# Attention's projections in three 16-bit passes, layer norm by four batches, value halves added in PSUM

## The chip, the cores and the metric

One core of a Trainium2 chip runs the whole kernel. The metric is the device time of one execution in microseconds, the median of the runs. TensorE (PE) multiplies matrices into PSUM, VectorE (DVE), ScalarE (ACT) and GpSimd (POOL) do the rest, SyncE (SP) issues the DMAs. Each engine works through its own list in order and waits on semaphores.

## The reference

```python
x = x + tanh(g_xattn[0]) * xattn(layernorm(x), ctx_768, Wq, Wk, Wv, Wo)
x = x + tanh(g_ffn[0]) * ffn(layernorm(x), W1, b1, W2, b2)

# xattn: 16 heads of 16
q, k, v = x @ Wq, context @ Wk, context @ Wv
out = softmax(q k^T / 4 (masked)) v        # per head
return out @ Wo
# ffn: ternary weights, exact gelu
h = gelu(x @ ternary(W1).T + b1); return h @ ternary(W2).T + b2
```

x is 128 batches x 128 rows x 256, the context 128 x 128 x 192, the hidden width of the feed-forward part 1024. Everything is float32.

## The kernel before

The attention stage takes two batches as a group (class Group), 64 groups in all; a loop body holds two groups, of parity 0 and 1. The feed-forward stage follows and takes four batches a step. The order on each engine is written out by hand: pe_group (L436), act_group (L625), dve_group (L834), pool_group (L917) and sp_group (L233) give each engine's list for one group, and interleave the end of one group, the middle of this one and the projections of later ones.

A group on TensorE is made of slots. A slot has rough_scores of four heads (L328, q against k with 16 rows), from which VectorE takes a maximum for each row (take_max, L744); scores of four heads (L352, 50 rows: high and low halves and the maximum), from which ScalarE makes exponentials (L596) and GpSimd their low half (L914); and weigh of four heads (L372 high and L373 low half of the probabilities, against v16 with 33 columns: 16 of the high half of v, 16 of its low half and a column of ones). Between them stand the projections in fp32, q (L296) and k (L305) of the group after next, v (L312) of the next one, in a bank that all three share (pj_bank), and the output projection (L391) of each batch. The transposes of x (L275), of the context (L285, L287), of the row maxima (transpose_max, L338) and of the attention output (L381) and the output projection share another bank, tr_bank; each waits until the bank's last content was read.

ScalarE copies the transposed tiles to SBUF (copy_xT L539, copy_ctxT L546, copy_attnT L604) and makes the 16-bit high halves of q, k and v (L559, L567, L576); VectorE makes the low halves (L707, L714, low_v L735). At the end of a group ScalarE's list has copy_attnT of the group's first batch and then high_v of the next group; project_out of that batch comes in the next group, after rough scores, scores and weigh of one slot. VectorE sums and scales the weighed values (read_weighed L773 and L774, normalise L782), once for each half of the heads, and adds the projected output to the residual (add_attention, L789).

The layer norm is worked out in 14 parts (ln_part, L657), spread over dve_group: statistics (bn_stats, L668), an inverse root by three Newton steps on columns of two numbers, a shift. It runs once for each group of two batches. The feed-forward stage uses the same function by four batches.

## Time and profile before

| | us |
|---|---|
| median of three runs | 1853.07 (1853.0 to 1859.49) |
| span of the profiled execution, first to last instruction | 1838.7 |
| PE busy | 1761.7 |
| DVE busy | 1538.3 |
| ACT busy | 952.2 |
| POOL busy | 661.2 |

The profile is of one execution. A run's time includes what lies before the first and behind the last instruction, so its median stands 14.4 us above the span of the profiled execution. Matmuls are pipelined: a row's length is that of the instruction from its start to the end of its result, and the pace is read from one start to the next. The timeline merges like instructions that follow one another ("x4"). The granted clock is the share of its full 2.4 GHz that TensorE was given.

### The profile page before, as it was taken

The numbers are of one execution on the slowest core, as the hardware profiler recorded it, in microseconds if no ns is written. First come the engines' busy times: TensorE is split into PE (matmuls) and PEld (weight loads), VectorE is DVE, ScalarE is ACT, GpSimd is POOL, SyncE is SP. The second block draws the span as 40 slices with busy tenths as digits, with TensorE's granted clock in tenths as the row PEclk, the third lists the DMA queues.
The fourth block names the chain that finished last, engine by engine and source line by source line (L and its number), as shares of the span: only waits on it lengthen the run. The fifth ranks groups of instructions, "written<-read, shape, count | busy, mean of one in ns | idle before, by whom it ended". The sixth has DMA issues, their size and how long they took to land.

```text
span 1838.7 us, 47676 instructions
## 1 busy us (share of the span) xinstructions
PE 1761.7 (96%) x14501; PEld 1152.8 (63%) x14501; DVE 1538.3 (84%) x4375; ACT 952.2 (52%) x1799; POOL 661.2 (36%) x809
## 2 busy tenths in 40 slices
PE   6999999999999999999999999999799999999998
PEld 3666666666666666666666666666466666666665
DVE  6799798898888988888898888987788888888886
ACT  3455555554555555555555555544455555555554
POOL 2344454454444444444444444545211111111111
PEclk9699898898988988898898888987699999999999
DMA  3222222222222222222222222221101110001011
GB/s 98 59 65 74 55 64 68 60 64 69 59 59 59 74 59 59 74 59 59 69 64 59 71 58 59 75 53 36 50 24 35 34 34 31 26 34 34 34 34 47
DMA packets 170607, 101.13 MB, mean 55 GB/s; under 512 B 20817, under 2 KB 170321, under 8 KB 170577
## 3 DMA queue, kind: packets, MB, share of 16 engines
q1 hardware_dynamic: 170576, 100.75, 20.0%
q8 instruction: 17, 0.28, 0.1%
q14 instruction: 14, 0.11, 0.0%
HBM read 32.53 MB, written 16.78 MB: 27 GB/s over the span
## 4 chain that ended last, share of the span: by engine, by line
PE 84%; DVE 8%; issue 5%; ACT 2%; DVEq 0%; DMA 0%; ACTq 0%
PE bank L1059 11%; PE bank L312 10%; PE bank L352 9%; PE bank L328 9%; PE bank L305 8%; PE bank L391 8%; PE bank L296 8%; PE bank L372 5%; PE bank L1089 5%; PE bank L1088 5%; PE bank L373 2%; PE bank L381 2%; DVE smax L759 2%; DVE y L1046 2%; PE bank L285 1%
## 5 line engine op out<-in xcount | busy, mean ns | idle before, releaser
L914 POOL TENSOR_TENSOR probl<-prob 128x512 f16<-128x512 f32 x512 | 531.6, 1044 | 712.5 <-ACT prob L596 710.9
L596 ACT ACTIVATE prob<-bank,masks 128x512 f32<-128x512 f32 x512 | 344.6, 686 | 314.3 <-PE bank L352 301.8
L744 DVE TENSOR_REDUCE smax<-bank 128x4 f32<-128x512 f32 x512 | 348.5, 682 | 46.1 <-PE bank L328 46.0
L1075 DVE TENSOR_TENSOR hidl<-hid 128x512 f16<-128x512 f32 x256 | 226.7, 886 | 79.4 <-ACT hid L1070 78.7
L1059 PE MATMUL bank<-y,w1T 128*128 128x512 f16 x1024 | 263.0, 379 | 29.7 <-DVE y L1046 28.2
L1070 ACT ACTIVATE hid<-bank,b_sb 128x512 f32<-128x512 f32 x256 | 175.8, 687 | 212.2 <-PE bank L1059 205.9
L1088 PE MATMUL bank<-w2T,hid 128*128 128x256 f16 x1024 | 237.4, 273 | 1.4 <-ACT w2T L1003 1.4
L1089 PE MATMUL bank<-w2T,hidl 128*128 128x256 f16 x1024 | 237.4, 273 | 0.0
L1153 POOL TENSOR_TENSOR xres<-xres,b2g 128x1024 f32 (+1 forms) x32 | 75.5, 2361 | 431.3 <-ACT yln L1023 413.4
L328 PEld LDWEIGHTS bank<-k_rows,q_rows 16*128 16x128 f16 x2048 | 120.5, 96 | 160.2 <-issue 128.2
L352 PE MATMUL bank<-q_rows,k_rows 50*128 50x128 f16 x2048 | 216.5, 230 | 0.9 <-DMA q_rows<-smaxT 0.9
L328 PE MATMUL bank<-k_rows,q_rows 16*128 16x128 f16 x2048 | 213.7, 227 | 1.7 <-DVE smax L744 1.7
L312 PE MATMUL bank<-wv_sb,ctxT 128*128 128x256 f32 (+1 forms) x512 | 195.7, 486 | 0.9 <-DVE k L714 0.9
L372 PE MATMUL bank<-v,prob 128*128 128x33 f16 x2048 | 178.2, 183 | 0.1
L373 PE MATMUL bank<-v,probl 128*128 128x33 f16 x2048 | 170.5, 179 | 0.0
L391 PE MATMUL bank<-wo_sb,attnT 128*128 128x256 f32 x512 | 166.7, 455 | 1.1 <-ACT attnT L604 1.1
L296 PE MATMUL bank<-xlnT,wq_sb 128*128 128x256 f32 x512 | 164.2, 451 | 2.0 <-DVE v L735 1.3
L372 PEld LDWEIGHTS bank<-v,prob 128*128 128x128 bf16 x2048 | 126.6, 98 | 59.9 <-issue 13.4
L1059 PEld LDWEIGHTS bank<-y,w1T 128*128 128x128 f16 x1024 | 97.5, 98 | 103.9 <-issue 33.1
L352 PEld LDWEIGHTS bank<-q_rows,k_rows 50*128 50x128 f16 x2048 | 121.9, 98 | 60.6 <-issue 12.6
L305 PE MATMUL bank<-ctxT,wk_sb 128*128 128x256 f32 (+1 forms) x512 | 159.0, 418 | 0.8 <-ACT ctxT L547 0.8
L373 PEld LDWEIGHTS bank<-v,probl 128*128 128x128 f16 x2048 | 131.2, 98 | 0.3 <-issue 0.3
(88 smaller groups left out, 2645.0 us busy)
## 6 DMA issues: line engine op xcount, KB each, us to landing
q_rows<-q SPq DMA_DIRECT2D x384, 64.0 KB, 2.6
k_rows<-k SPq DMA_DIRECT2D x384, 64.0 KB, 2.5
xres<-in_x_dram SPq DMA_DIRECT2D x64, 256.0 KB, 2.8
out_dram<-ystage SPq DMA_DIRECT2D x32, 512.0 KB, 2.9
ctx_sb<-in_ctx_dram SPq DMA_DIRECT2D x64, 192.0 KB, 2.9
q_rows<-smaxT SPq DMA_DIRECT2D x128, 8.0 KB
w_raw<-in_L_ffn_W_dram SPq DMA_DIRECT2D x2, 1024.0 KB, 6.6
prob<-in_L_xattn_Wq_dram SPq DMA_DIRECT2D x1, 256.0 KB, 4.0
```

What stands on the lines that cost most here:

```text
L312: last = pe.matmul(pj_bank[:, b * D:(b + 1) * D], ctxT[g.parity][0:rows, k, b * S:(b + 1) * S], wv_sb[0:rows, k, :], start=(k == 0), stop= ...
L328: last = pe.matmul(sm_bank[u % 2][:, c * S:(c + 1) * S], q_rows[g.parity][0:HD, b, u * UH + c, :], k_rows[g.parity][0:HD, b, u * UH + c, : ...
L352: last = pe.matmul(st_bank[u % 2][:, c * S:(c + 1) * S], k_rows[g.parity][0:SR, b, u * UH + c, :], q_rows[g.parity][0:SR, b, u * UH + c, : ...
L372: pe.matmul(o, high, v, start=True, stop=False)
L373: last = pe.matmul(o, probl[u][:, c * S:(c + 1) * S], v, start=False, stop=True)
L391: last = pe.matmul(tr_bank[:, 0:D], attnT[:, k, :], wo_sb[:, k, :], start=(k == 0), stop=(k == KD - 1))
L596: act.activation(prob[u][:], st_bank[u % 2][:], ACT.Exp, bias=0.0, scale=masks[g.parity][:, 2 + b:3 + b]).then_inc(exp_done, 1)
L744: dve.tensor_reduce(smax[:, b, u * UH:(u + 1) * UH], sm_bank[u % 2][:].rearrange("p (h j) -> p h j", h=UH), AX.X, ALU.max).then_inc(max_ta ...
L914: pool.tensor_tensor(probl[u][:], prob[u][:], prob[u][:].bitcast(BF16)[:, 1::2], ALU.subtract).then_inc(prob_split, 1)
L1059: last = pe.matmul(h_bank[f % 2][:], w1T[:, k, f * P:(f + 1) * P], y16[g.parity][:, part, k, :], start=(i == 0), stop=(i == 2 * KD - 1))
L1088: pe.matmul(o, high, w2T[:, f, :], start=(f == 0 and b % 2 == 0), stop=False, skip_group_check=True)
L1089: last = pe.matmul(o, hidl[f % HBUF][:, b * S:(b + 1) * S], w2T[:, f, :], start=False, stop=(f == FB - 1), skip_group_check=True)
```

## The change

- The four projections take 16-bit high and low halves of both operands, in three passes (high x high, high x low, low x high), where one fp32 matmul stood. The weights are scaled by 64 and split once, ahead of the first group (high_weights on ScalarE, low_weights on VectorE). The context is cut as 96 + 96 rows, not 128 + 64.
- ScalarE's copies of the transposed x, context and attention output now write the high half; VectorE writes the low half (low_x, low_ctx, low_attn). The projections, and whoever uses tr_bank next, wait for the low half.
- low_q and low_k are one instruction each, not two; q and k lie in PSUM by batch.
- weigh multiplies each half of the probabilities by each half of v, to the same 17 columns of PSUM: four matmuls a head of 17, 16, 17 and 16 columns, not two of 33. One bank holds a whole batch, so VectorE reads it once a batch (sum_weighed, normalise) and the reduction over the halves is gone.
- The layer norm of x runs once for two groups, by four batches, in groups of parity 0; x is loaded by four batches.
- The order of pe_group and act_group stays. In dve_group low_attn of the last group's first batch stands behind norm(0) at the start.

```diff
+            if g.parity == 1 and left >= 6:
+                sp.wait_ge(ln_ready, x_past)
+                load_x(sp, g.half + 3)
             if left >= 3:
...
+        def by_batch(m):
+            return pj_bank[:].rearrange("p (b m s) -> p m b s", m=KD, b=2)[:, m]
         def project_q(pe, g, m):
             if m == 0:
-                pe.wait_ge(xT_copied, g.n + 1)
+                pe.wait_ge(xT_split, g.n + 1)
             for k in range(KD):
-                last = pe.matmul(pj_bank[:, m * T:(m + 1) * T], wq_sb[:, k, m * P:(m + 1) * P],
-                                 xlnT[:, k, :], start=(k == 0), stop=(k == KD - 1))
+                for i, (wp, xp) in enumerate(SPLIT):
+                    last = pe.matmul(by_batch(m), wq16[:, wp, k, m * P:(m + 1) * P],
+                                     xT16[:, xp, k, :].rearrange("p (b s) -> p b s", b=2),
+                                     start=(k == 0 and i == 0 and m == 0), stop=(k == KD - 1 and i == 2),
+                                     skip_group_check=True)
             if m == KD - 1:
                 last.then_inc(q_made, 1)
...
         def project_v(pe, g, b):
-            for k, rows in enumerate((P, C1)):
-                last = pe.matmul(pj_bank[:, b * D:(b + 1) * D], ctxT[g.parity][0:rows, k, b * S:(b + 1) * S],
-                                 wv_sb[0:rows, k, :], start=(k == 0), stop=(k == 1))
+            for k in range(2):
+                for i, (wp, xp) in enumerate(SPLIT):
+                    last = pe.matmul(pj_bank[:, b * D:(b + 1) * D], ctxT16[g.parity][:, xp, k, b * S:(b + 1) * S],
+                                     wv16[:, wp, k, :], start=(k == 0 and i == 0 and b == 0),
+                                     stop=(k == 1 and i == 2), skip_group_check=True)
             if b == 1:
                 last.then_inc(v_made, 1)
...
                 pe.wait_ge(v_split, g.n + 1)
-            if u % 2 == 0 and not (isinstance(n, int) and n == 0):
-                pe.wait_ge(norm_read, n * 2 + (half - 1))
+            if u == 0 and not (isinstance(n, int) and n < 2):
+                pe.wait_ge(norm_done, n - 1)
             for c in range(UH):
-                o = pv_bank[half][:, (c0 + c) * VC:(c0 + c + 1) * VC]
-                v = v16[g.parity][:, b, u * UH + c, :]
+                h = u * UH + c
+                o = pv_bank[b][:, h * VH:(h + 1) * VH]
                 high = prob[u][:].bitcast(BF16)[:, 2 * c * S + 1:2 * (c + 1) * S:2]
-                pe.matmul(o, high, v, start=True, stop=False)
-                last = pe.matmul(o, probl[u][:, c * S:(c + 1) * S], v, start=False, stop=True)
+                low = probl[u][:, c * S:(c + 1) * S]
+                vh, vl = v16[g.parity][:, b, h, 0:VH], v16[g.parity][:, b, h, VH:VC]
+                pe.matmul(o, high, vh, start=(h == 0), stop=False, skip_group_check=True)
+                pe.matmul(o[:, 0:HD], high, vl, start=False, stop=False, skip_group_check=True)
+                pe.matmul(o, low, vh, start=False, stop=False, skip_group_check=True)
+                last = pe.matmul(o[:, 0:HD], low, vl, start=False, stop=(h == HEADS - 1), skip_group_check=True)
             last.then_inc(weighed, 1)
...
         def project_out(pe, n, tr_free):
             for busy in tr_free:
                 pe.wait_ge(*busy)
-            pe.wait_ge(attnT_copied, n + 1)
+            pe.wait_ge(attnT_split, n + 1)
             for k in range(KD):
-                last = pe.matmul(tr_bank[:, 0:D], attnT[:, k, :], wo_sb[:, k, :], start=(k == 0),
-                                 stop=(k == KD - 1))
+                for i, (wp, xp) in enumerate(SPLIT):
+                    last = pe.matmul(tr_bank[:, 0:D], attnT16[:, xp, k, :], wo16[:, wp, k, :],
+                                     start=(k == 0 and i == 0), stop=(k == KD - 1 and i == 2))
             last.then_inc(projected, 1)
             return [(x1_done, n + 1)]
...
         def copy_ctxT(act, g):
             act.wait_ge(ctx_transposed, g.n + 1)
             if not (isinstance(g.half, int) and g.n < 2):
                 act.wait_ge(v_made, g.n - 1)
-            act.copy(ctxT[g.parity][:, 0, :], tr_bank[:, 0:T])
-            act.copy(ctxT[g.parity][0:C1, 1, :], tr_bank[0:C1, T:2 * T]).then_inc(ctxT_copied, 1)
...
+        def high_weights(act):
+            act.wait_ge(weights_in, 16 * 4)
+            for i, (raw, w) in enumerate(((wq_raw, wq16), (wk_raw, wk16), (wv_raw, wv16), (wo_raw, wo16))):
+                for k in range(2):
+                    if i >= 2:
+                        last = act.activation(w[:, 0, k, :], raw[:, k, :], ACT.Identity, bias=0.0, scale=WS)
+                        continue
+                    for m in range(KD):
+                        last = act.activation(permuted(w[:, 0, k], m), permuted_raw(raw[:, k], m), ACT.Identity,
+                                              bias=0.0, scale=WS)
+                last.then_inc(weights_high, 1)
...
+        def norm_x(dve, half, parts):
             for i in parts:
                 if i == 0:
-                    dve.wait_ge(x_in[g.parity], 16 * (g.half + 1))
-                if i == 3 and not (isinstance(g.half, int) and g.n == 0):
-                    dve.wait_ge(ln_done, 2 * g.n)
-                rows = [row_of(g.batch(b)) for b in range(2)] if i == 0 else (None,) * 2
-                ln_part(dve, i, rows, ln_step, g.n * (LN_PARTS - 1), ln_ready)
+                    dve.wait_ge(x_in, 16 * (half + 1))
+                if i == LN_PARTS - 2 and not (isinstance(half, int) and half == 0):
+                    dve.wait_ge(ln_done, QB * half)
+                rows = [row_of(half * QB + b) for b in range(QB)] if i == 0 else ()
+                ln_part(dve, i, rows, ln_step, half * (LN_PARTS - 1), ln_ready)
...
+        def low_x(dve, g):
+            dve.wait_ge(xT_high, g.n + 1)
+            dve.tensor_tensor(xT16[:, 1].rearrange("p k t -> p (k t)"), tr_bank[:],
+                              xT16[:, 0].rearrange("p k t -> p (k t)"), ALU.subtract).then_inc(xT_split, 1)
+        def low_ctx(dve, g):
+            dve.wait_ge(ctxT_high, g.n + 1)
+            dve.tensor_tensor(ctxT16[g.parity][:, 1].rearrange("p k t -> p (k t)"), tr_bank[0:CK, :],
+                              ctxT16[g.parity][:, 0].rearrange("p k t -> p (k t)"),
+                              ALU.subtract).then_inc(ctxT_split, 1)
+        def low_attn(dve, n):
+            dve.wait_ge(attnT_high, n + 1)
+            dve.tensor_tensor(attnT16[:, 1].rearrange("p k t -> p (k t)"), tr_bank[:, 0:KD * S],
+                              attnT16[:, 0].rearrange("p k t -> p (k t)"), ALU.subtract).then_inc(attnT_split, 1)
...
         def low_q(dve, g):
             dve.wait_ge(q_high, g.n + 1)
-            for b in range(2):
-                last = dve.tensor_tensor(q16[g.parity][:, 1, b], by_batch(pj_bank)[:, b], q16[g.parity][:, 0, b],
...
+        def low_weights(dve):
+            for i, (raw, w) in enumerate(((wq_raw, wq16), (wk_raw, wk16), (wv_raw, wv16), (wo_raw, wo16))):
+                dve.wait_ge(weights_high, i + 1)
+                for k in range(2):
+                    if i >= 2:
+                        last = dve.scalar_tensor_tensor(w[:, 1, k, :], raw[:, k, :], WS, w[:, 0, k, :], ALU.mult,
+                                                        ALU.subtract)
+                        continue
+                    for m in range(KD):
+                        last = dve.scalar_tensor_tensor(permuted(w[:, 1, k], m), permuted_raw(raw[:, k], m), WS,
+                                                        permuted(w[:, 0, k], m), ALU.mult, ALU.subtract)
+                last.then_inc(weights_split, 1)
...
+        def sum_weighed(dve, n, b):
+            dve.wait_ge(weighed, (n + 1) * UNITS)
             if not (isinstance(n, int) and n < 2):
                 dve.wait_ge(attn_transposed, n - 1)
-            pv = pv_bank[half][:, 0:HB * VC].rearrange("p (h c) -> p h c", h=HB)
-            dve.reciprocal(rsum[:, b, heads], pv[:, :, 2 * HD])
-            dve.tensor_reduce(attn[b][:, heads, :],
-                              pv[:, :, 0:2 * HD].rearrange("p h (two d) -> p h d two", two=2), AX.X,
-                              ALU.add).then_inc(norm_read, 1)
-        def normalise(dve, n, b, half):
-            heads = slice(half * HB, (half + 1) * HB)
-            dve.wait_ge(norm_read, n * 2 + (half + 1))
-            dve.tensor_tensor(attn[b][:, heads, :], attn[b][:, heads, :],
-                              rsum[:, b, heads].unsqueeze(2).to_broadcast([P, HB, HD]),
+            dve.reciprocal(rsum[:, b, :], pv_of(b)[:, :, HD]).then_inc(norm_read, 1)
+        def normalise(dve, n, b):
+            dve.wait_ge(norm_read, n + 1)
+            dve.tensor_tensor(attn[b][:], pv_of(b)[:, :, 0:HD],
+                              rsum[:, b, :].unsqueeze(2).to_broadcast([P, HEADS, HD]),
                               ALU.mult).then_inc(norm_done, 1)
...
-            norm_x(dve, g1, range(LN_PARTS))
+            low_x(dve, g0)
+            low_weights(dve)
             low_q(dve, g0)
             dve.wait_ge(gates_set, 1)
+            dve.tensor_scalar(gates[:, 0:1], gates[:, 2:3], 1.0 / WS, None, ALU.mult).then_inc(gate_scaled, 1)
+            low_ctx(dve, g0)
             low_k(dve, g0)
-            norm_x(dve, g0.after(2), range(0, LN_AHEAD))
+            low_x(dve, g1)
+            norm_x(dve, 1, range(0, LN_PARTS - 2))
             low_v(dve, g0)
-            norm_x(dve, g0.after(2), range(LN_AHEAD, LN_PARTS))
+            norm_x(dve, 1, range(LN_PARTS - 2, LN_PARTS))
+            low_ctx(dve, g1)
             low_q(dve, g1)
...
             first = isinstance(g.half, int) and g.n == 0
-            g1, g2, g3, g4 = (g.after(k) for k in range(1, 5))
+            g1, g2 = g.after(1), g.after(2)
             def norm(i):
                 if left == 0:
-                    norm_y(dve, Group(0, 0), ((i - LN_AHEAD) % LN_PARTS,))
-                if i < LN_AHEAD and left >= 4:
-                    norm_x(dve, g4, (i,))
-                if i >= LN_AHEAD and left >= 3:
-                    norm_x(dve, g3, (i,))
+                    norm_y(dve, Group(0, 0), (i,))
+                if g.parity == 0 and left >= 4:
+                    norm_x(dve, g.half + 2, (i,))
+            norm(0)
+            if not first:
+                low_attn(dve, g.batch(0) - 2)
             take_max(dve, g, 1, 2)
-            norm(8)
             if not first:
                 add_attention(dve, g.batch(0) - 2)
-            norm(9)
+            norm(1)
             take_max(dve, g, 1, 3)
             round_max(dve, g, 1)
-            norm(10)
+            norm(2)
             low_max(dve, g, 1)
+            norm(3)
             if not first:
-                read_weighed(dve, g.batch(0) - 1, 1, 1)
-                normalise(dve, g.batch(0) - 1, 1, 1)
-            norm(11)
+                sum_weighed(dve, g.batch(0) - 1, 1)
+                norm(4)
+                normalise(dve, g.batch(0) - 1, 1)
+            else:
+                norm(4)
             if left >= 2:
+                low_ctx(dve, g2)
                 low_q(dve, g2)
-            norm(12)
+            norm(5)
             if left >= 1:
                 take_max(dve, g1, 0, 0)
-            norm(13)
+            norm(6)
             if left >= 1:
                 take_max(dve, g1, 0, 1)
-            read_weighed(dve, g.batch(0), 0, 0)
-            normalise(dve, g.batch(0), 0, 0)
+            norm(7)
+            if not first:
+                low_attn(dve, g.batch(0) - 1)
             if left >= 1:
                 take_max(dve, g1, 0, 2)
+            norm(8)
             if left >= 2:
                 low_k(dve, g2)
+            norm(9)
             if not first:
                 add_attention(dve, g.batch(0) - 1)
+            norm(10)
             if left >= 1:
                 take_max(dve, g1, 0, 3)
                 round_max(dve, g1, 0)
+                norm(11)
                 low_max(dve, g1, 0)
-            norm(0)
-            read_weighed(dve, g.batch(0), 0, 1)
-            norm(1)
-            normalise(dve, g.batch(0), 0, 1)
-            norm(2)
+            else:
+                norm(11)
...
             if left >= 1:
                 take_max(dve, g1, 1, 1)
-            norm(4)
-            read_weighed(dve, g.batch(1), 1, 0)
...
```

## Rows read from the trace of the kernel before

**Rows 1.** The page: busy shares of the span, and the granted clock in 40 slices.

```profile
PE 1761.7 (96%) x14501; PEld 1152.8 (63%) x14501; DVE 1538.3 (84%) x4375; ACT 952.2 (52%) x1799; POOL 661.2 (36%) x809
...
PEclk9699898898988988898898888987699999999999
```

**Rows 2.** Timeline of TensorE (start us, length us, engine, line, operation): L338.

```profile
587.45 0.23 PE L338 MATMUL bank<-ident,smax 128*32 128x128 f16 x1
...
642.01 0.23 PE L338 MATMUL bank<-ident,smax 128*32 128x128 f16 x1
...
666.11 0.23 PE L338 MATMUL bank<-ident,smax 128*32 128x128 f16 x1
...
684.19 0.23 PE L338 MATMUL bank<-ident,smax 128*32 128x128 f16 x1
...
706.89 0.23 PE L338 MATMUL bank<-ident,smax 128*32 128x128 f16 x1
```

**Rows 3.** Windows (stretch, length; busy of PE, PEld, DVE, ACT, POOL; clock; DMA).

```profile
586.00:650.80 64.80, 63.86 (x626) 41.47 (x625) 58.74 (x168) 37.90 (x76) 32.10 (x45) 1.00 0.25 65
650.80:664.50 13.70, 13.70 (x72) 8.46 (x72) 9.43 (x33) 3.83 (x9) 4.02 (x4) 0.50 0.22 63
695.20:705.40 10.20, 10.20 (x51) 6.58 (x51) 7.12 (x22) 3.35 (x8) 3.12 (x3) 0.50 0.31 84
1330.00:1830.00 500.00, 471.37 (x3281) 321.18 (x3282) 411.61 (x1122) 267.88 (x440) 73.19 (x31) 1.00 0.09 32
```

**Rows 4.** Timeline of TensorE, 603 to 610 us, full clock.

```profile
603.62 1.03 PE L296 MATMUL bank<-xlnT,wq_sb 128*128 128x256 f32 x4
...
604.58 0.39 PE L328 MATMUL bank<-k_rows,q_rows 16*128 16x128 f16 x4
...
606.81 2.48 PE L305 MATMUL bank<-ctxT,wk_sb 128*128 128x256 f32 x8
...
609.22 0.39 PE L328 MATMUL bank<-k_rows,q_rows 16*128 16x128 f16 x4
```

**Rows 5.** Timeline of TensorE, two matmuls of one weigh, six steps apart.

```profile
618.32 0.18 PE L373 MATMUL bank<-v,probl 128*128 128x33 f16 x1
...
618.47 0.18 PE L373 MATMUL bank<-v,probl 128*128 128x33 f16 x1
```

**Rows 6.** Timeline of TensorE in the feed-forward stage, matmuls seven steps apart.

```profile
1505.51 0.27 PE L1088 MATMUL bank<-w2T,hid 128*128 128x256 f16 x1
...
1506.27 0.27 PE L1089 MATMUL bank<-w2T,hidl 128*128 128x256 f16 x1
```

**Rows 7.** Timeline of TensorE, ScalarE and VectorE, 616 to 620 us.

```profile
616.47 1.22 PE L312 MATMUL bank<-wv_sb,ctxT 128*128 128x256 f32 x4
...
617.62 0.39 PE L328 MATMUL bank<-k_rows,q_rows 16*128 16x128 f16 x4
...
617.87 0.85 ACT L576 ACTIVATE v<-bank,masks 128x256 f16<-128x256 f32 x2 [0.81 <-PE bank L312]
...
618.49 1.11 PE L391 MATMUL bank<-wo_sb,attnT 128*128 128x256 f32 x4
...
618.75 0.88 DVE L735 SCALAR_TENSOR_TENSOR v<-bank,masks,v 128x256 f16<-128x256 f32 x2 [0.53 <-ACT v L576]
...
619.53 0.39 PE L328 MATMUL bank<-k_rows,q_rows 16*128 16x128 f16 x4
```

**Rows 8.** Groups of instructions by line and shape (count; busy us, mean ns; idle before).

```profile
L668 DVE BATCH_NORM_STATS2 stats<-xres 128x6 f32 x228 | 82.4, 413 | 0.0
...
L1046 DVE TENSOR_TENSOR y<-bank,y 128x512 f16<-128x512 f32 x64 | 40.9, 677 | 0.1
```

**Rows 9.** Timeline of TensorE at L338, with the idle time before it.

```profile
692.61 0.22 PE L338 MATMUL bank<-ident,smax 128*32 128x128 f16 x1 [0.35 <-DVE smax L759]
```

**Rows 10.** Timeline of TensorE at half clock: four rough scores, then four scores.

```profile
697.22 0.60 PE L328 MATMUL bank<-k_rows,q_rows 16*128 16x128 f16 x4
...
697.75 0.60 PE L352 MATMUL bank<-q_rows,k_rows 50*128 50x128 f16 x4
```

More of the change, by code:

```diff
@@ L657, in ln_part @@
         def ln_part(dve, i, rows, step, base, ready):
-            n = len(rows)
-            half, y, t, shift = (rstd[:, k, 0:n] for k in range(4))
+            half, y, t = (rstd[:, k, :] for k in range(3))
             if i > 0:
@@ L1010, in norm_y @@
             for i in parts:
[L1011 to L1014 removed]
+                if i == LN_PARTS - 2:
+                    if isinstance(g.half, int) and g.n == 0:
+                        dve.wait_ge(ln_done, B)
+                    else:
+                        dve.wait_ge(y_done, QB * g.n)
+                rows = [row_of(g.n * QB + b) for b in range(QB)] if i == 0 else ()
                 ln_part(dve, i, rows, y_step, g.n * (LN_PARTS - 1), y_ready)
```

216 lines of the change are left out of this document (107 added, 109 removed).

## The prediction

> **What bounds the kernel now.** I read the page first: TensorE is busy for 96% of the span, VectorE for 84%, and the granted TensorE clock is below full in most slices of the first two thirds, full in the last third [rows 1]. The attention stage fills about 1270 us of the span, as 64 groups of two batches. Then I read the timeline of TensorE at one instruction that comes once in a group, the transpose of the row maxima at L338 (it has two a group, so every second one stands there). Three groups in a row take 587.45 to 642.01, 18.19 us each, at full clock. The next takes 24.10 us, and one soon after 22.70 us; six groups take 119.44 us, 19.91 each [rows 2]. The view by windows says what the long ones are: for 13.70 us (650.80 to 664.50) and 10.20 us (695.20 to 705.40) the granted clock is 0.50, that is 1.2 GHz in place of 2.4, with TensorE busy all the time; the feed-forward stage, denser 256 and 512 column matmuls, holds 1.00 throughout [rows 3]. So a group is bounded by TensorE's own in-order stream, and a drop of the clock costs (24.10 - 18.19) = 5.9 and (22.70 - 18.19) = 4.5 us, 1.7 us a group over six groups. VectorE is no bound as a sum, but it runs its list in order, and TensorE waits for single items of it.
>
> **TensorE's work, removed.** One project_q half (four fp32 matmul instructions) takes 603.62 to 604.58, 0.96 us; project_k 606.81 to 609.22, 2.41 [rows 4]; one project_v half 616.47 to 617.62, 1.15, and one project_out 618.49 to 619.53, 1.04 [rows 7]. A group has two q halves, one k, two v halves and two outputs: 1.92 + 2.41 + 2.30 + 2.08 = 8.7 us. The change makes them 48 passes of 256 columns on 16-bit data. Such a pass stands in the feed-forward stage: seven in a row start 0.76 us apart, 109 ns each [rows 6]. 48 x 0.109 = 5.2 us, and I add 0.1 us at each of seven ends, because project_out's 1.04 us are 0.17 more than its eight 109 ns column passes and part of that is the changeover to a matmul with other rows. So 5.9, a saving of **2.8 us a group**. Bounds: 3.5 without changeover, 2.3 with 0.17 each.
>
> **TensorE's work, added.** weigh has 8 matmuls of 33 columns for four heads now, and will have 16 of 17 or 16 columns. The present ones start 25 ns apart (618.32 to 618.47 for six steps) [rows 5], although 33 columns at 2.4 GHz are 14 ns: the step is not set by columns, so halving the columns brings nothing. 8 more x 25 ns x 8 units = **1.6 us a group**. Bounds: 1.6, and 0.9 if a step fell to the 14 ns. Net of both: -1.2 us a group. That is all the gain there is, some 75 us over the stage.
>
> **VectorE's work.** It loses two reductions and half of its small instructions on [128 x 8] sums a batch, and half of the Newton steps, since four batches share them; it gains low_x and low_ctx (512 columns from PSUM, as the 677 ns of the row at L1046 [rows 8]) and two low_attn (256 columns, about 0.42). As a sum it gets lighter, so it is nothing on the path. What counts is where the new items stand.
>
> **The new wait.** project_out now waits for attnT_split, which low_attn gives, and low_attn of a group's first batch stands in VectorE's list behind low_v of the same point and, in every even group, behind the four bn_stats of norm(0). low_v waits for high_v on ScalarE, and that for project_v. Follow this in the trace: project_v ends at 617.62, high_v starts at 617.87, low_v at 618.75 and takes 0.88 [rows 7]; low_attn adds 0.42 and the signal 0.1. From the end of project_v: 0.25 + 0.88 + 0.88 + 0.42 + 0.1 = 2.5 us. In even groups four bn_stats of 413 ns [rows 8], back to back some 0.34 each, make it 3.9. TensorE needs it much sooner: today project_out starts 618.49 - 617.62 = 0.87 us after project_v, and with the longer weigh 1.07. So it stands idle for 1.45 us in odd groups and 2.85 in even ones, **2.15 us a group**; before, the copy on ScalarE that fed it came ahead of high_v. Behind the waiting instruction are the rough scores and scores that feed VectorE's maxima and ScalarE's exponentials, so nothing of the next slot can fill the hole. Bounds: 1.1 if low_v were already further on, 3.0 if one small instruction more stretches. A smaller wait of the same kind: transpose_max stands idle already, 0.35 us at 692.61 for VectorE's low half of the maxima [rows 9]; low_x of 0.68 comes behind it and gives the bank free, and low_ctx does the same for the other transpose_max. weigh's added time hides part; I take 0.6 us a group for the two (bounds 0 and 1.3). Loads of x come as four batches in half as many DMAs and are early; they cost nothing.
>
> **Sum at full clock:** 18.19 - 1.2 + 2.15 + 0.6 = 19.7 us a group.
>
> **The clock.** The falls come where TensorE's stream is thin: the one at 695.20 [rows 3] follows, by 2.6 us, on the idle time at L338 [rows 9], with the 16-row rough scores and the 33-column matmuls between. The change thins exactly that place: an idle stretch of 1.45 to 2.85 us beside rough scores and 17-column matmuls, and the projections, the densest part, shrink from 8.7 to 5.9 us. Two groups in six meet a fall today; I expect one in every group. A fall costs 0.43 us per us at half clock today (5.9 of 13.7); with more waiting in the stream, which the clock doesn't stretch, I take 4.3 us a group. 19.7 + 4.3 = **24.0 us a group**. Against 19.91: 4.1 x 62 groups (the first two run while the pipeline fills) = 254 us. The start adds the scaling and splitting of all four weight matrices on ScalarE and VectorE before the first project_q, some 24 instructions of about 0.3 us, partly beside each other: 6 us. The feed-forward stage is unchanged. Span 1838.7 + 260 = 2099; the median of the runs is 14.4 us above the span of the profiled execution, so **2113 us**.
>
> **Rivals.**
> 1. The wait comes, the clock doesn't fall oftener. For: TensorE is 98 to 100% busy in the stage today and its clock falls all the same, so idle time isn't the sole trigger; the walk doesn't say what is. Against: what is thinned is what precedes the falls. Price: 19.7 + 1.7 = 21.4 a group, +1.5 x 62 + 6 = +99: **1952**. Beside this the Trainium skill (TensorE: Matmul & The Clock Gate, "Why this matters for your kernels") blames drops on idle gaps between bursts longer than any wait worked out here, which would give this case; the trace disagrees with it as the only cause, for the clock is 0.50 right after a stretch with 63.86 of 64.80 us busy [rows 3].
> 2. The clock, once down, stays down for most of the stage, since 16-bit projections leave no stretch as dense as fp32's. A group wholly at half clock: rough and real scores 16 x 0.53 (697.22 to 697.75 [rows 10]) = 8.5, projections 5.9 x 1.9 = 11.2, weigh 3.9, transposes 3.8, waits 1.0: 28.4. (28.4 - 19.91) x 62 + 6 = +532: **2385**. Today it recovers within 14 us, in q's or the fp32 stretches.
> 3. The wait is hidden and the sum of TensorE's work decides: -1.2 x 62 + 6 = -68: **1785**. It would take low_v finishing some 1.5 us sooner after project_v than the 2.0 us that the trace shows; I find nothing that gives that.
> 4. Saving, wait and clock cancel: within 0.5% of 1853.
>
> **How the numbers follow.** Chances: forecast 0.58 (2000 to 2240 by its bounds), rival 1 0.17, rival 2 0.13, rival 3 0.08, rival 4 0.04. The range 1880 to 2300 leaves out rivals 3 and 4 and most of rival 2. Faster by over 0.5% (what a measurement can tell from no change) 0.08, within 0.04, slower 0.88.
>
> **What would show it.** In the profile after: project_out idle before its first matmul, released by VectorE's low_attn, 1 to 3 us a time, longer in every second group; weigh's matmuls 25 ns apart; projection passes 109 ns apart at full clock; the granted clock at 0.50 for 30 to 60% of the attention stage. I am wrong if the mean granted clock there stays near 0.90 (today 23.9 of 119.44 us at half), or if project_out starts without idle time.

## The result and the profile after

The changed kernel takes **2220.88 us** (2201.32 to 2225.24, four runs) against 1853.03 for the kernel before on the same chip: a ratio of 1.199, 95% interval [1.192, 1.205]. The forecast was 2113 in a range of 1880 to 2300, slower.

First the page of the changed kernel, the lines that answer to [rows 1].

```profile
span 2214.9 us, 55976 instructions
...
PE 2050.9 (93%) x19621; PEld 1404.8 (63%) x19621; DVE 1378.3 (62%) x3549; ACT 974.8 (44%) x1747; POOL 660.0 (30%) x809
...
PEclk9555555555555566655555555556556999999999
```

VectorE's busy time fell by 160 us, and TensorE's rose by 289. The granted clock, mostly 8 to 9 tenths before, reads 5, in some slices 6, in the attention stage; the feed-forward stage at the end is as it was. The windows say it in numbers (stretch, length; busy of PE, PEld, DVE, ACT, POOL; clock; DMA); the first five lie each within a single stretch at one level of the clock and all but fill it, then come 1000 us of the stage and the feed-forward stage.

```profile
100.60:110.90 10.30, 9.77 (x153) 7.34 (x152) 8.91 (x23) 6.88 (x13) 5.78 (x9) 1.00 0.16 41
110.90:151.80 40.90, 38.15 (x358) 25.69 (x358) 20.36 (x53) 14.74 (x27) 12.22 (x16) 0.50 0.19 53
343.00:411.20 68.20, 63.42 (x603) 42.87 (x602) 36.16 (x99) 25.61 (x47) 21.16 (x27) 0.50 0.18 46
619.50:622.80 3.30, 3.30 (x59) 2.71 (x59) 2.63 (x7) 2.46 (x6) 0.93 (x1) 1.00 0.01 2
623.00:674.00 51.00, 48.24 (x455) 32.17 (x452) 25.80 (x68) 19.17 (x36) 16.91 (x23) 0.50 0.20 49
150.00:1150.00 1000.00, 939.80 (x9839) 645.95 (x9838) 565.98 (x1432) 418.73 (x775) 348.02 (x465) 0.59 0.19 48
1705.00:2213.00 508.00, 475.98 (x3322) 324.54 (x3319) 415.60 (x1128) 270.48 (x443) 73.53 (x32) 1.00 0.10 33
```

For comparison the kernel before over the same 1000 us:

```profile
150.00:1150.00 1000.00, 988.30 (x8733) 637.55 (x8732) 856.55 (x2508) 527.74 (x1054) 452.94 (x602) 0.90 0.24 63
```

Before, the clock went to 0.50 for 10 to 14 us at a time and was back; now it is at 0.50 for 41 or 51 us at most times, once for 68, and back at 1.00 for 10 or 3. A mean of 0.59 is 1.2 GHz for (1 - 0.59) / 0.5 = 82% of the stage. From one transpose of row maxima to the next but one (L354, the measure of [rows 2]) a group takes 25.9 us on average over 56 groups (19.8 before), with none under 22.8.

The timeline of the changed kernel at the end of an odd group (parity 1), at half clock, shows the wait that the prediction worked out; it answers to [rows 7].

```profile
713.26 1.49 PE L327 MATMUL bank<-wv,ctxT 96*128 96x256 f16 x6
...
714.92 0.85 ACT L599 ACTIVATE v<-bank,masks 128x256 f16<-128x256 f32 x2 [1.04 <-PE bank L327]
...
715.80 0.88 DVE L799 SCALAR_TENSOR_TENSOR v<-bank,masks,v 128x256 f16<-128x256 f32 x2 [3.19 <-ACT v L599]
...
716.60 1.40 DVE L701 BATCH_NORM_STATS2 stats<-xres 128x6 f32 x4
...
717.91 0.41 DVE L752 TENSOR_TENSOR attnT<-bank,attnT 128x256 f16<-128x256 f32 x1
...
718.37 1.46 PE L411 MATMUL bank<-wo,attnT 128*128 128x256 f16 x6 [2.03 <-DVE attnT L752]
```

project_v (L327) ends at 714.68, where the next rough scores (L344) start; high_v (L599) ends at 715.77, low_v (L799) at 716.68, the four bn_stats (L701), grouped in one line, at 718.00, low_attn (L752) at 718.32, and project_out starts at 718.37 after 2.03 us of idle time. From 714.68 that is 3.69 us, where 3.9 was worked out. In the other groups, without bn_stats, the same place reads:

```profile
688.44 0.88 DVE L799 SCALAR_TENSOR_TENSOR v<-bank,masks,v 128x256 f16<-128x256 f32 x2 [3.20 <-ACT v L599]
...
689.23 0.41 DVE L752 TENSOR_TENSOR attnT<-bank,attnT 128x256 f16<-128x256 f32 x1
...
689.70 1.46 PE L411 MATMUL bank<-wo,attnT 128*128 128x256 f16 x6 [0.72 <-DVE attnT L752]
```

Idle times of 0.72 and 2.03 us alternate through the whole stage. In total (engine and line that waited, whom for; us in total, times, longest):

```profile
PE bank L411 <- DVE attnT L752: 86.1, 65, 2.0
...
PE bank L354 <- DVE xT L741: 9.2, 23, 1.1
```

The other terms can be read off as well. weigh's matmuls, 14 steps apart at full clock, then 13 steps apart at half clock (start, length):

```profile
101.21 0.17 PE L390 MATMUL bank<-v,prob 128*128 128x16 f16 x1
...
101.56 0.17 PE L392 MATMUL bank<-v,probl 128*128 128x16 f16 x1
```

```profile
706.64 0.17 PE L390 MATMUL bank<-v,prob 128*128 128x16 f16 x1
...
706.98 0.18 PE L391 MATMUL bank<-v,probl 128*128 128x17 f16 x1
```

25 ns a step at full clock, as the 33 columns were [rows 5], and 26 to 27 at half. Here the Trainium skill (TensorE: Matmul & The Clock Gate, "Wait — 56ns, not 53.3ns?") states that starts are never closer than about 25 ns however few the columns; the trace agrees for 16, 17 and 33 columns at full clock, and between the two levels of the clock the step of 16 and 17 columns moves by 1 to 2 ns only. The projection of k, twelve passes of 256 columns, first at full and then at half clock:

```profile
103.15 1.48 PE L317 MATMUL bank<-ctxT,wk 96*128 96x256 f16 x12
104.56 0.39 PE L344 MATMUL bank<-k_rows,q_rows 16*128 16x128 f16 x4
```

```profile
699.92 2.77 PE L317 MATMUL bank<-ctxT,wk 96*128 96x256 f16 x12
702.62 0.60 PE L344 MATMUL bank<-k_rows,q_rows 16*128 16x128 f16 x4
```

1.41 us and 2.70 us, 0.117 and 0.225 a pass with the changeover. The fp32 form took 2.41 at full clock [rows 4]. So both terms of TensorE's own work came out as summed: the projections got shorter, weigh longer.

### The profile page after: what moved, and what is told of

Its sections match the earlier page's. It is cut to its first block, busy times and chain, and to the rows that moved or that the text cites. A ratio compares the mean times of both kernels' runs of the same rounds, so it can differ in the third digit from the quotient of the medians.

```text
span 2214.9 us, 55976 instructions
## 1 busy us (share of the span) xinstructions
PE 2050.9 (93%) x19621; PEld 1404.8 (63%) x19621; DVE 1378.3 (62%) x3549; ACT 974.8 (44%) x1747; POOL 660.0 (30%) x809
## 4 chain that ended last, share of the span: by engine, by line
PE 77%; DVE 10%; issue 8%; ACT 3%; DVEq 1%; DMA 0%; ACTq 0%; SPq 0%
PE bank L344 9%; PE bank L1123 9%; PE bank L368 8%; PE bank L305 7%; PE bank L327 7%; PE bank L411 6%; PE bank L317 6%; PE bank L1152 4%; PE bank L1153 4%; PE bank L389 4%; PE bank L400 3%; PE bank L290 2%; PE bank L391 2%; PE bank L279 2%; PE bank L390 2%
## 5 line engine op out<-in xcount | busy, mean ns | idle before, releaser
L344 PE MATMUL bank<-k_rows,q_rows 16*128 16x128 f16 x2048 | 281.0, 281 | 1.8 <-DVE smax L808 1.8
L368 PE MATMUL bank<-q_rows,k_rows 50*128 50x128 f16 x2048 | 280.4, 281 | 0.7 <-DMA q_rows<-smaxT 0.7
L389 PEld LDWEIGHTS bank<-v,prob 128*128 128x128 bf16 x2048 | 209.9, 103 | 87.9 <-issue 73.5
L344 PEld LDWEIGHTS bank<-k_rows,q_rows 16*128 16x128 f16 x2048 | 158.4, 117 | 165.2 <-issue 152.8
L389 PE MATMUL bank<-v,prob 128*128 128x17 f16 x2048 | 262.3, 179 | 0.0
L391 PE MATMUL bank<-v,probl 128*128 128x17 f16 x2048 | 251.6, 174 | 0.0
L390 PE MATMUL bank<-v,prob 128*128 128x16 f16 x2048 | 251.0, 174 | 0.0
L392 PE MATMUL bank<-v,probl 128*128 128x16 f16 x2048 | 250.8, 173 | 0.0
L411 PE MATMUL bank<-wo,attnT 128*128 128x256 f16 x768 | 170.7, 388 | 86.1 <-DVE attnT L752 86.1
L390 PEld LDWEIGHTS bank<-v,prob 128*128 128x128 bf16 x2048 | 214.6, 105 | 0.1
L391 PEld LDWEIGHTS bank<-v,probl 128*128 128x128 f16 x2048 | 208.8, 102 | 0.0
L392 PEld LDWEIGHTS bank<-v,probl 128*128 128x128 f16 x2048 | 208.2, 102 | 0.0
```

Source lines behind the costliest of these rows:

```text
L344: last = pe.matmul(sm_bank[u % 2][:, c * S:(c + 1) * S], q_rows[g.parity][0:HD, b, u * UH + c, :], k_rows[g.parity][0:HD, b, u * UH + c, : ...
L368: last = pe.matmul(st_bank[u % 2][:, c * S:(c + 1) * S], k_rows[g.parity][0:SR, b, u * UH + c, :], q_rows[g.parity][0:SR, b, u * UH + c, : ...
L389: pe.matmul(o, high, vh, start=(h == 0), stop=False, skip_group_check=True)
L390: pe.matmul(o[:, 0:HD], high, vl, start=False, stop=False, skip_group_check=True)
L391: pe.matmul(o, low, vh, start=False, stop=False, skip_group_check=True)
L392: last = pe.matmul(o[:, 0:HD], low, vl, start=False, stop=(h == HEADS - 1), skip_group_check=True)
```

## The experiments

The theories before the runs: **A**, the idle time at project_out brings the clock down; **B**, the thinner matmuls in weigh do. When the first four had been read, two more: **C**, the clock falls where too few dense columns pass (matmuls of many rows and many columns, one right behind the other), and the shorter projections took the densest; **D**, the short waits that are still left in e4 (at the transposes, for instance) hold the clock down. The last three runs ask for the two together. All runs stand in one table; "clock" is the mean over 150 to 1150 us of each profile, "group" the mean time of 56 groups. The kernel before ran again beside each set of experiments (1849 to 1854 us), and each ratio is to those runs.

| run | us | ratio to before, 95% | clock | group us |
|---|---|---|---|---|
| before | 1849 to 1854 | 1 | 0.90 | 19.8 |
| after | 2220.9 | 1.199 [1.192, 1.205] | 0.59 | 25.9 |
| e1_low_attn_first | 2024.2 | 1.093 [1.089, 1.098] | 0.66 | 22.8 |
| e2_before_wait | 2077.0 | 1.119 [1.110, 1.127] | 0.76 | 23.7 |
| e3_old_weigh | 2048.7 | 1.107 [1.102, 1.112] | 0.66 | 23.2 |
| e4_both | 1926.8 | 1.042 [1.038, 1.047] | 0.68 | 21.4 |
| e5_four_passes | 1885.2 | 1.019 [1.015, 1.023] | 0.85 | 20.5 |
| e6_both_filler | 1897.0 | 1.025 [1.018, 1.032] | 0.76 | 20.9 |
| e7_before_filler | 1849.7 | 1.001 [0.998, 1.005] | 0.96 | 19.8 |
| e8_after_filler | 2358.4 | 1.273 [1.266, 1.280] | 0.54 | 28.4 |
| e9_before_split_weigh | 1910.0 | 1.034 [1.030, 1.038] | 0.91 | 20.9 |
| e10_filler_late_max | 1840.8 | 0.993 [0.989, 0.998] | 0.90 | 19.5 |
| e12_before_late_max | 1891.2 | 1.023 [1.019, 1.026] | 0.91 | 20.6 |
| e13_late_max_only | 1946.4 | 1.053 [1.045, 1.062] | 0.70 | 21.6 |

### The wait alone, in the kernel before (e2_before_wait)

```diff
                 weigh(pe, before, 1, 2)
+                pe.wait_ge(v_split, g.n + 1)
                 tr = project_out(pe, g.batch(0) - 2, tr)
```

> The kernel before with one wait added and nothing else: project_out of a group's first batch also waits for low_v of the same point (v_split). By the rows of before that idles TensorE by 0.25 + 0.88 + 0.88 - 0.87 = 1.1 to 1.3 us a group. Theory A: the idle time brings a fall of the clock in nearly every group, at 4 to 5 us each: 23 to 25 us a group, 2030 to 2150 us. Theory B: only the wait's own time, 64 x 1.2 = 77 us, and falls as often as before: 1910 to 1950 us.

2077.0 us, +228 for one line. TensorE's idle time for it (waits view, then the window):

```profile
PE bank L391 <- DVE v L736: 57.3, 63, 1.1
```

```profile
150.00:1150.00 1000.00, 954.82 (x7281) 609.98 (x7282) 701.88 (x2098) 438.92 (x880) 378.94 (x499) 0.76 0.20 53
```

57.3 us is 0.9 us a group; the group grew by 3.9 (23.7 for 19.8). TensorE's time not busy grew by as much as the wait, from 0.23 us a group (11.7 us in 1000) to 1.07 (45.2 in 1000); the other 3 us it spends busy, on the same matmuls, at a clock of 0.76 for 0.90. Nothing else in the kernel is changed, and no single wait in the 1000 us is longer than 1.1 us. This is theory A, shown. The section of the Trainium skill that the prediction weighed (TensorE: Matmul & The Clock Gate, "Why this matters for your kernels") blames longer gaps than these; the trace does not agree with it as the only cause.

### The wait taken out of the changed kernel (e1_low_attn_first)

```diff
             norm(0)
-            if not first:
-                low_attn(dve, g.batch(0) - 2)
             take_max(dve, g, 1, 2)
...
                 take_max(dve, g1, 1, 1)
+                low_attn(dve, g.batch(0))
                 low_v(dve, g1)
```

> The changed kernel with one thing moved: on VectorE low_attn of a group's first batch stands ahead of low_v, not behind low_v and norm(0). Theory A (the wait at project_out is what brings the clock down): the wait of 1.3 us a time at project_out goes, the granted clock of the stage rises from 0.59 to 0.85 or more, a group takes 19 to 20.5 us in place of 26, the kernel 1800 to 1900 us. Theory B (the thinner matmuls bring it down, the 16 and 17 column weigh and the shorter projections): the wait goes, the clock stays under 0.70, and the kernel wins no more than the wait's own time, 64 x 1.3 to 2.2 us: 2080 to 2140 us.

```profile
PE bank L411 <- DVE attnT L752: 2.0, 2, 1.0
...
PE bank L354 <- DVE xT L741: 10.2, 35, 0.4
```

```profile
150.00:1150.00 1000.00, 988.37 (x11125) 692.60 (x11123) 627.96 (x1622) 470.75 (x874) 393.83 (x526) 0.66 0.21 55
```

The wait is gone (2.0 us in total, from 86.1), and 197 us with it, more than twice what was idle; but the clock comes back only to 0.66, and the kernel lands between what A and B had expected. The wait is a cause, and not the only one. TensorE now stands idle for 11.6 us of the 1000, as little as in the kernel before (11.7), and the clock is 0.66 against 0.90. How long TensorE waits does not explain what is left of the loss; its work, the passes and weigh, is what still differs.

### weigh undone, and both (e3_old_weigh, e4_both)

```diff
-                pe.matmul(o, high, vh, start=(h == 0), stop=False, skip_group_check=True)
-                pe.matmul(o[:, 0:HD], high, vl, start=False, stop=False, skip_group_check=True)
-                pe.matmul(o, low, vh, start=False, stop=False, skip_group_check=True)
-                last = pe.matmul(o[:, 0:HD], low, vl, start=False, stop=(h == HEADS - 1), skip_group_check=True)
+                pe.matmul(o, high, v, start=True, stop=False)
+                last = pe.matmul(o, probl[u][:, c * S:(c + 1) * S], v, start=False, stop=True)
```

(with read_weighed and normalise of the kernel before, in VectorE's list at its places there; e4 has this and the order of e1).

> The changed kernel with weigh and its reading undone: two matmuls of 33 columns a head, halves added by VectorE, as in the kernel before; low_attn stays behind low_v. Theory A: the wait at project_out stays (and grows by some 0.2 us), the clock stays under 0.70; the group loses 1.6 us of weigh: 2050 to 2130 us. Theory B: half of the thinning goes, the clock rises to 0.75 to 0.85: 1930 to 2020 us.

> The changed kernel with both: low_attn ahead of low_v, and weigh as in the kernel before. Left of the change are the three 16-bit passes and the layer norm by four batches. Theory A and B alike: no long wait, the weigh as dense as before; at full clock 18.2 - 2.8 + 0.5 = 16 us a group; with falls as often as before 17.6 us: 1690 to 1760 us. If the shorter projections alone keep the clock low (theory C), it stays under 0.75 and the kernel takes over 1850 us.

e3 is where A put it, at the lower edge: 2049 us at a clock of 0.66. e4 is a miss for A and B: without the wait at project_out and with the old weigh it should have been faster than before, and it is 4% slower, at 0.68. Short waits are left in it, 40.1 us of the 1000, the longest 0.9. The windows of e3 and e4:

```profile
150.00:1150.00 1000.00, 905.17 (x8219) 611.89 (x8218) 749.91 (x1941) 459.41 (x868) 391.08 (x518) 0.66 0.20 55
...
150.00:1150.00 1000.00, 959.90 (x8831) 650.30 (x8827) 805.35 (x2086) 492.01 (x931) 418.53 (x555) 0.68 0.22 58
```

The old weigh is worth 97 us without the wait (e1 to e4), about what its steps cost (1.6 us a group, some 100 us in all), and the clock moves only from 0.66 to 0.68. With the wait in place it is worth 172 us (after to e3), and the clock moves from 0.59 to 0.66 although TensorE stands idle longer, 94.8 us of the 1000 for 60.2. So in these kernels the thinner weigh costs more than its steps where the long wait stands beside it.

What e4 still has of the change is the layer norm by four batches and the three 16-bit passes, with the context cut as 96 + 96 rows. So theory C: the passes. It can be tried by adding work.

### weigh's change alone, in the kernel before (e9_before_split_weigh)

The change's weigh, sum_weighed and normalise put into the kernel before, with its layout of the values:

```diff
-                pe.matmul(o, high, v, start=True, stop=False)
-                last = pe.matmul(o, probl[u][:, c * S:(c + 1) * S], v, start=False, stop=True)
+                pe.matmul(o, high, vh, start=(h == 0), stop=False, skip_group_check=True)
+                pe.matmul(o[:, 0:HD], high, vl, start=False, stop=False, skip_group_check=True)
+                pe.matmul(o, low, vh, start=False, stop=False, skip_group_check=True)
+                last = pe.matmul(o[:, 0:HD], low, vl, start=False, stop=(h == HEADS - 1), skip_group_check=True)
...
-            read_weighed(dve, g.batch(0), 0, 1)
+            sum_weighed(dve, g.batch(0), 0)
```

> The kernel before with the change's weigh and its reading alone: four matmuls of 17 and 16 columns a head, halves added in PSUM, one reciprocal and one scaling a batch; fp32 projections and the layer norm as before. By the sum 8 x 8 x 25 ns = 1.6 us more a group at full clock: 18.2 + 1.6 = 19.8. Theory C (density decides the clock): weigh's stretches are longer and thinner, so falls come oftener than two in six groups, 19.8 + 2.5 to 4.5: 22.3 to 24.3 us a group, 2010 to 2140 us. If falls stay as they are: 21.5 a group, 1950 to 1970 us.

```profile
150.00:1150.00 1000.00, 1000.00 (x11410) 681.27 (x11411) 653.12 (x2011) 510.39 (x1006) 431.57 (x575) 0.91 0.23 61
```

```profile
536.14 0.23 PE L339 MATMUL bank<-ident,smax 128*32 128x128 f16 x1
...
594.22 0.23 PE L339 MATMUL bank<-ident,smax 128*32 128x128 f16 x1
```

Three groups at full clock take 594.22 - 536.14 = 58.08 us, 19.36 each against 18.19 [rows 2]: +1.2, where 1.6 was summed. The clock stays at 0.91. My expectation for theory C was wrong at this point, and 1910 us is also below the 1950 for falls as before: thin stretches in weigh do not by themselves bring the clock down. They cost their 25 ns steps: with 1849.0 for the kernel before on the same chip, 61 us in all. One thing helps them here: behind the longer weigh the wait at transpose_max is gone, and TensorE is not idle at all in the 1000 us (11.7 before). Theory B is out as an account of the whole; that weigh matters beside a long wait, e3 shows.

### More work, less time (e5_four_passes, e6_both_filler)

```diff
-        SPLIT = ((0, 0), (0, 1), (1, 0))
+        SPLIT = ((0, 0), (0, 1), (1, 0), (1, 1))
```

> Like e4_both, with the fourth pass of every projection (low x low) kept: 64 passes of 256 columns a group in place of 48, 16 x 0.109 = 1.7 us more work at full clock. Theory C (the clock follows how densely 128-row columns fill TensorE's stream, and the shorter projections thinned it): the clock of the stage rises from 0.68 to 0.80 or more and the kernel gets faster for having more work: 1800 to 1890 us. Theory D (the short waits left in e4_both, 0.3 to 1 us at transpose_max, transpose_x and project_out, hold the clock down): clock as in e4_both, 1927 + 64 x (1.7 to 3) = 2040 to 2100 us.

```profile
150.00:1150.00 1000.00, 950.38 (x9980) 682.91 (x9978) 846.55 (x2176) 510.24 (x969) 436.78 (x580) 0.85 0.23 61
```

A third more projection passes, 16 x 0.109 = 1.7 us more a group at full clock, and the kernel is 42 us faster than e4: the clock goes from 0.68 to 0.85. The waits at transpose_max did not shrink, they grew; the same rows of the waits view, e4 and then e5:

```profile
PE bank L354 <- DVE xT L738: 15.0, 31, 0.9
...
PE bank L354 <- DVE ctxT L743: 9.8, 12, 0.9
```

```profile
PE bank L354 <- DVE xT L738: 33.7, 61, 2.6
...
PE bank L354 <- DVE ctxT L743: 13.2, 29, 0.8
```

That speaks against D: 46.9 us of these waits at a clock of 0.85, 24.8 at 0.68. And e5 is back to short falls: no stretch at 0.50 in its 1000 us is longer than 13.7 us, as in the kernel before, where e4 has stretches up to 44 us. A long stretch of e4, and a fall of e5 with the 48 us at full clock behind it:

```profile
523.30:564.20 40.90, 40.22 (x299) 26.20 (x299) 30.19 (x78) 16.65 (x32) 14.53 (x19) 0.50 0.21 57
```

```profile
470.20:483.70 13.50, 13.50 (x94) 9.04 (x91) 9.11 (x20) 4.04 (x8) 3.72 (x4) 0.50 0.29 83
483.80:531.50 47.70, 44.47 (x551) 33.02 (x549) 42.74 (x109) 27.72 (x54) 23.97 (x33) 1.00 0.24 61
```

e6 puts extra columns somewhere else, one overwritten matmul ahead of each four rough scores:

```diff
+            for _ in range(1):
+                pe.matmul(sm_bank[u % 2][:, 0:D], wq16[:, 0, 0, 0:P], wq16[:, 0, 0, :], start=True, stop=True)
             for c in range(UH):
                 last = pe.matmul(sm_bank[u % 2][:, c * S:(c + 1) * S],
```

> Like e4_both, with one matmul of 128 rows and 256 columns that does nothing (it is overwritten) ahead of each four rough scores, the thinnest place of a slot: 8 x 0.109 = 0.9 us more work a group at full clock. Theory C: the clock rises to 0.90 or more; a group takes about 17 us, the kernel 1690 to 1760 us. Theory D: the clock stays near 0.68, 1927 + 64 x (0.9 to 1.7) = 1985 to 2040 us.

1897 us, 30 faster than e4 for 0.9 us more work a group, at 0.76. The sign is as C says (D had 1985 or more); the size is not, C had 1690 to 1760.

### The filler in the kernel before and in the changed one (e7_before_filler, e8_after_filler)

```diff
+            for _ in range(2):
+                pe.matmul(sm_bank[u % 2][:, 0:P], ident16[:], ident16[:], start=True, stop=True)
```

(e7; two of 128 columns ahead of each four rough scores. e8 is e6's single matmul of 256 columns, put into the changed kernel.)

> The kernel before with two matmuls of 128 rows and 128 columns that do nothing ahead of each four rough scores: 8 x 0.11 = 0.9 us more work a group, nothing else changed. Theory C: the falls of before go (clock 0.97 or more in the stage), a group takes 18.2 + 0.9 = 19.1 us in place of 19.8: 1795 to 1825 us, faster than before. Theory D: falls as before, 1850 + 57 = 1895 to 1920 us.

> The changed kernel with the same filler of 256 columns ahead of each four rough scores; the wait at project_out stays. Theory C: the clock rises from 0.59 to 0.65 to 0.80, since the idle stretch at project_out still thins the stream: 2080 to 2190 us. Theory D: clock as in the changed kernel, 2221 + 64 x (0.9 to 1.7) = 2280 to 2330 us.

e7: the clock rises to 0.96, groups take 19.1 us one after another with a fall now and then, and what the clock gives back is what the filler costs: 1849.7 us, the same as before, between what C (1795 to 1825) and D (1895 to 1920) had expected. e8 is a miss for both: 2358 us, 138 more than without the filler, at 0.54. Beside the idle stretch at project_out this filler does not bring the clock back, and it is only paid for, at half clock most of the time. Why the clock falls a little further, from 0.59 to 0.54, was not tried. The windows of e7 and e8:

```profile
150.00:1150.00 1000.00, 1000.00 (x9641) 672.21 (x9642) 834.21 (x2542) 532.93 (x1063) 460.01 (x611) 0.96 0.24 64
```

```profile
150.00:1150.00 1000.00, 958.71 (x9203) 648.85 (x9200) 507.74 (x1307) 380.94 (x702) 317.21 (x421) 0.54 0.17 45
```

### The row maxima's transpose moved (e10, e12, e13)

```diff
             weigh(pe, g, 0, 0)
-            tr = transpose_max(pe, g, 1, tr)
             if left >= 1:
                 rough_scores(pe, g1, 0, 1)
             scores(pe, g, 0, 3)
+            tr = transpose_max(pe, g, 1, tr)
...
             if left >= 1:
-                tr = transpose_max(pe, g1, 0, tr)
...
             scores(pe, g, 1, 3)
+            if left >= 1:
+                tr = transpose_max(pe, g1, 0, tr)
             weigh(pe, g, 1, 1)
```

ScalarE's copies of the maxima and the next exponentials change places to match. e12 is this edit in the kernel before, e13 in e4, and e10 in e6.

> Like e6_both_filler, with transpose_max (and ScalarE's copy of it) moved later by one rough_scores and one scores, so that TensorE has work while VectorE finishes low_x and low_ctx. In e6 it stood idle 0.3 to 0.9 us there and the clock fell near these places. Theory C': density and these waits together decide; without the waits the clock stays up, 0.90 or more, 16.8 us a group: 1690 to 1770 us. If the waits only move to the next instruction that uses the bank: as e6, 1870 to 1900 us.

> The kernel before with transpose_max and ScalarE's copy of it moved later in the same way, nothing else. Before, TensorE idles 0.35 us a group at it and the falls of the clock follow by 2 to 3 us. Theory C: without that idle time the stream of before is dense enough and the falls go: 18.2 us a group less 0.3, 1720 to 1760 us, faster than before. If the idle time there has no part in the falls: 1820 to 1850 us.

> Like e4_both, with transpose_max moved later as in e10_filler_late_max and without the filler; it completes a square of four kernels (neither: e4, 1927 us; filler: e6, 1897 us; later maximum: this one; both: e10, 1841 us). If the idle time at transpose_max is what keeps the clock down in e4, this one has a clock near e10's 0.91 and 0.9 us a group less work: 1770 to 1800 us. If the density of the work itself decides, the clock stays under 0.80 and it takes 1870 to 1930 us.

With e4 and e6 these make a square: neither 1927, filler alone 1897, later transpose alone 1946, both 1841. The move by itself costs 20 us, the filler by itself gains 30, and both together gain 86. All three runs missed: e10 lies between its two ranges, e12 above both of its own (1891 us for 1820 to 1850 at most), e13 above both of its own (1946 for 1870 to 1930 at most). e13 has 2 waits over 0.6 us in its 1000 us where e4 has 25, and its clock stays at 0.70, so idle time at transpose_max is not what holds it down, and theory D falls with it; with the filler the same move brings 0.90 where the filler alone had 0.76. The move also has a price of its own: in the kernel before it costs 42 us (e12), since the next transposes of attn (L381) now wait until ScalarE has copied the maxima out of their common bank. The windows of e10, of e12 and of e13, and this wait in e12:

```profile
150.00:1150.00 1000.00, 918.81 (x10134) 648.50 (x10132) 866.04 (x2302) 549.39 (x1024) 459.31 (x613) 0.90 0.25 64
...
150.00:1150.00 1000.00, 960.04 (x8489) 622.62 (x8487) 834.75 (x2438) 527.33 (x1025) 441.06 (x586) 0.91 0.24 62
...
150.00:1150.00 1000.00, 948.74 (x8842) 644.26 (x8841) 798.85 (x2088) 499.62 (x932) 418.32 (x556) 0.70 0.23 59
```

```profile
PE bank L381 <- ACT smaxT L587: 38.7, 92, 0.5
```

e12 and e13 are the closest pair that the runs have for the projections. Both have the old weigh, the late transpose and no wait in the 1000 us longer than 0.63 us; TensorE is idle for 40.0 us in e12 and 51.3 in e13, and the clock is 0.91 with the fp32 projections and 0.70 with the three passes. The layer norm by four batches stands between them too, but it gives TensorE no instruction more or less and can reach it only by waits, which are nearly alike here.

The same rows limit what e2 showed. Idle time as a sum does not tell the clock: e10 is idle for 81.2 us of 1000, in pieces of at most 0.54, at 0.90, and e12 for 40.0 at 0.91, while e2 is idle for 45.2, mostly in pieces of 0.6 to 1.1 us, at 0.76. Whether the length of a piece or its place decides was not tried.

Why the filler and the later transpose gain more together than the sum of both is not settled.

e10 is the only version faster than the kernel before, by 0.7% [0.2, 1.1], and its runs spread from 1819 to 1916 us. Its filler matmuls are overwritten, so that it is a probe of the clock more than a version to keep.

## Why the prediction was right

**TensorE's work removed** and **added**: as summed. Passes are 109 ns apart at full clock, project_k's twelve take 1.41 us as the sum has it, and weigh's steps are 25 ns; weigh alone measured +1.2 us a group for a sum of 1.6 (e9), and where the other 0.4 went was not tried.

**VectorE's work**: lighter, as said; its busy time in the 1000 us shown fell from 857 to 566 us, in a group from 0.857 x 19.8 = 17.0 to 0.566 x 25.9 = 14.7.

**The new wait**: the chain was right item by item, 3.69 us against 3.9 from the end of project_v to project_out, and the alternation between groups with and without bn_stats. The size of the idle time, 0.72 and 2.03 us for 1.45 and 2.85, is smaller because the stage runs at half clock, where rough scores, scores and weigh cover 1.7 us of it and not 1.07. The waits at transpose_max, 0.6 us a group or 37 in all in the sum, are 9.2 us in the whole changed kernel, at half clock; in e5, at 0.85, they are 46.9. Both terms of waiting were too large for the stage as it ran.

**The clock** carried the forecast, and its term was mis-sized. I took one fall for each group, 4.3 us; the clock stood at 0.50 for 82% of the stage and not for 30 to 60%. The group took 25.9 us, which is 6.2 above the 19.7 summed at full clock, and 7.4 above 18.5, the same sum with the waits as measured (1.4 and 0.15 us). So the term of 4.3 us should have been 6 to 7, and the waits taken too large hid a part of that. 25.9 for 24.0 is 1.9 x 62 = 118 us, more than the 108 us between forecast and result. The reason I gave for the fall, idle time beside thin matmuls, holds for the idle time (e2: +228 us for a wait of 0.9 us a group), and for weigh only beside that idle time (e3), not alone (e9: clock 0.91). The shorter projections I had named as a part of the thinning; they weigh most of the rest (e4 at 0.68 with neither of the other two, e5 at 0.85 with a pass more, e13 at 0.70 beside e12 at 0.91). Rival 2 had the reason, no stretch left as dense as fp32's to bring the clock back: at 0.50 for 41 us on end where it was 14 before. Its price, a stage wholly at half clock, was 2385; the truth lies between it and the forecast. So the direction and the chain of the wait were right by their reasons, while the form of the clock's loss was rival 2's, not one fall for each group: that the result fell inside the range owes something to the room that the range left for it.

**Rival 1** (the clock falls no oftener, 1952) is ruled out by 0.59 for 0.90. **Rival 3** (the wait hidden) is ruled out as a fact, and e4, which comes near it as an experiment, shows that it would not have led to 1785 either: 1927.

Not settled: the layer norm by four batches was not tried alone, nor the three passes alone in the kernel before. By what VectorE's changed order makes TensorE wait for, a part of e4's loss could be the layer norm's, but in e1 TensorE waits no longer than in the kernel before, and its clock is low all the same. Nor was it tried apart whether the passes lower the clock by being fewer, by their 16-bit type or by the context's 96 rows; that a fourth one of the same kind undoes most of it points to their number. That the clock answers to waits of about 1 us at project_out and to the work taken from or added to TensorE is shown; by what rule it does is not.

## What to carry to other kernels

A stall of TensorE is priced by its own length only while the clock stays; in a stage where it falls already (here in two groups of six) 0.9 us more of waiting in a group, in one piece, cost 3.9, while as much idle time in shorter pieces at another place (e12) left the clock at 0.91. Before replacing fp32 matmuls by fewer 16-bit passes, look whether the dense stretches that go are what keeps the clock at 2.4 GHz, and where a new producer stands in the in-order list of its engine: here moving one instruction ahead of another (e1) was worth 197 us.

## What the runs showed of the hardware that I had not expected

- Adding work made kernels faster: a fourth projection pass by 42 us (e5 against e4), overwritten matmuls by 30 (e6 against e4) and, with a wait moved, by 106 (e10 against e13).
- The clock can stay at 1.2 GHz for 41 to 68 us with TensorE 93 to 95% busy all the while (38.15 of 40.90 us and 63.42 of 68.20 in the windows above).
- Idle time does not tell the clock: idle for 11.6 us of 1000 TensorE had 0.66 (e1), idle for 81.2 it had 0.90 (e10).
- Back-to-back matmuls of 16 and 17 columns keep nearly the same step at both levels of the clock, 25 and 26 to 27 ns; those of 256 columns stretch from 0.117 to 0.225 us a pass (project_k above).
